# Five engine queues of one kernel, the same instructions in another order

## The reference

```python
    x = L0_attn_x
    xn = _layernorm(x, axis=-1)
    s = _L0_attn_ref(xn, ...)        # Mamba: in_W, conv of 4, silu, dbc, softplus, scan over 256 steps, 16 states, silu gate, out_W
    g = _silu(_L0_ffn_ref(xn, ...))  # six layers:
    #   x = attn_layer(shift_tokens(x), Wqkv, ...) + x   16 heads of 64, l2norm of q and k, rotary, windows of 32
    #   x = ffn_layer(shift_tokens(x), ...) + x          layer norm, W1, a * gelu(gate), W2
    x = x + s * g
```

## Time and profile before

| | us |
|---|---|
| median of 3 runs | 1926.24 (1923.84 to 1934.32) |
| the profiled execution | 1930.3 |
| its span, first to last instruction | 1928.5 |
| busy PE / DVE / POOL / ACT in the span | 1756.7 / 1596.1 / 1527.8 / 1252.5 |

### The profile page before, as it was taken

The page is one execution under the profiler, slowest core; times in us unless marked ns, Lnnn a source line. Parts: engine busy times, 40 slices in busy tenths (PEclk is TensorE's granted clock), DMA queues, the critical chain, the costliest instruction groups (busy, mean ns, idle before and its releaser), DMA issues. The chain is left out here.

```text
span 1928.5 us, 73996 instructions
## 1 busy us (share of the span) xinstructions
PE 1756.7 (91%) x30944; PEld 999.4 (52%) x30944; DVE 1596.1 (83%) x2736; ACT 1252.5 (65%) x2339; POOL 1527.8 (79%) x1348
## 2 busy tenths in 40 slices
PE   3798999999999999999999999999999999999862
PEld 1355555555555555555555555555555555555420
DVE  5777998888888897889988898889878798888536
ACT  3566676676676676776776676676766666766630
POOL 1765899878998789878998789888888689987640
PEclk9999999999999999999999999999999999999975
DMA  3114234153313334142332433342331534123321
GB/s 109 29 39 70 45 71 79 37 85 49 66 33 67 72 61 71 41 71 55 68 71 37 87 49 59 74 79 39 67 58 33 100 62 63 30 45 58 54 23 44
DMA packets 95607, 113.14 MB, mean 59 GB/s; under 512 B 42334, under 2 KB 61548, under 8 KB 95276
## 3 DMA queue, kind: packets, MB, share of 16 engines
q1 hardware_dynamic: 95276, 108.41, 31.1%
HBM read 19.22 MB, written 1.05 MB: 11 GB/s over the span
## 5 line engine op out<-in xcount | busy, mean ns | idle before, releaser
L1315 POOL TENSOR_TENSOR AB<-qc,qn 128x512 f32<-128x512 f32 x384 | 494.6, 1298 | 21.4 <-DVE qn L1109 21.4
L1326 POOL TENSOR_TENSOR AB<-AB,rinv 128x512 f32<-128x512 f32 x384 | 402.0, 1062 | 24.5 <-DVE rinv L1132 24.5
L559 PE MATMUL bank<-wqkv,XT 128*128 128x512 f32 x768 | 400.2, 614 | 12.2 <-DVE qn L1109 12.2
L1333 POOL TENSOR_TENSOR Pb<-Pb,p_rden 128x512 f32<-128x512 f32 x192 | 200.1, 1042 | 235.2 <-DVE p_rden L1153 234.1
L848 ACT ACTIVATE qkT<-bank 128x512 f32<-128x512 f32 x384 | 229.2, 597 | 209.3 <-PE bank L584 208.6
L1109 DVE TENSOR_TENSOR qc<-bank,rt 128x512 f32<-128x512 f32 x384 | 261.3, 680 | 123.4 <-ACT sq L839 108.9
L584 PEld LDWEIGHTS bank<-ident,AB 128*128 128x128 f32 x1536 | 181.7, 142 | 181.9 <-issue 119.3
L839 ACT ACTIVATE sq<-bank 128x512 f32<-128x512 f32 x384 | 228.1, 594 | 66.4 <-PE bank L559 57.3
L1109 DVE TENSOR_TENSOR qn<-bank,rt 128x512 f32<-128x512 f32 x384 | 261.4, 681 | 0.0
L584 PE MATMUL bank<-ident,AB 128*128 128x128 f32 x1536 | 241.5, 280 | 13.3 <-ACT qkT L848 6.2
L1116 DVE TENSOR_REDUCE ssq<-sq 128x8 f32<-128x512 f32 x384 | 251.2, 670 | 0.0
(11 more groups left out here) (137 smaller groups left out, 2657.3 us busy)
## 6 DMA issues: line engine op xcount, KB each, us to landing
V<-V SPq DMA_DIRECT2D x672, 64.0 KB, 2.1
rep<-du SPq DMA_DIRECT2D x64, 512.0 KB, 7.3
wqkv<-in_Wqkv SPq DMA_DIRECT2D x36, 256.0 KB, 3.7
XV<-XT SPq DMA_DIRECT2D x96, 64.0 KB, 2.8
wo<-in_Wo SPq DMA_DIRECT2D x6, 512.0 KB, 4.1
BC<-BC SPq DMA_DIRECT2D x8, 256.0 KB
w<-in_W SPq DMA_DIRECT2D x6, 341.0 KB, 3.2
BC<-BC SPq DMA_DIRECT2D x8, 128.0 KB
```

The costliest lines, as they stand in the source:

```text
L559: pe.matmul(R[u % 2][:], XT[:, s % NB, (u % 2) * P:(u % 2 + 1) * P], wqkv[:, (u // 2) * 512:(u // 2 + 1) * 512], start=True, stop=True).th ...
L1315: pool.tensor_tensor(AB[:, n % NAB, :], qc[:, u % 2, :], qn[:, u % 2, :], ALU.add).then_inc(rs_done, 1)
L1326: pool.tensor_tensor(o, o, r, ALU.mult).then_inc(nm_done, 1)
L1333: pool.tensor_tensor(Pb[:, g % 2], Pb[:, g % 2], r, ALU.mult).then_inc(pn_done, 1)
```

## The change

Each of the five loops gets its lines in another order, and `M_ORDER` follows. No call is added or dropped, no instruction, tile, buffer or semaphore changes. Some calls move by an iteration, so that their argument changes: `z_softplus` runs for step i-1 instead of i-2, the ACT call `z_copy_dbc` stands at the end of the list with i instead of further up with i-1, two `z_scan`, some `z_bu` and some `replicate` move likewise. Lines that the prediction speaks of, cut from the diff:

```diff
@@ M_ORDER @@
-M_ORDER = [("z_x", 0, -1, 6), ("z_dbc", 0, 1, 6), ("z_out", 0, 9, 6), ("z_g", 0, 5, 6), ("z_dup", 0, 1, 6),
+M_ORDER = [("z_dbc", 0, 1, 6), ("z_x", 0, -1, 6), ("z_dup", 0, 1, 6), ("z_out", 0, 9, 6), ("z_g", 0, 5, 6),
...
@@ block.sync @@
             for i in FIRST_TO_LAST:
+                replicate_bc(i - 3, 0)
+                spread(i, 0)
                 replicate(i - 4, 2)
-                next_qk(i, 1)
-                replicate(i - 7, 5)
-                replicate_bc(i - 3, 0)
-                replicate(i - 6, 4)
-                replicate_bc(i - 4, 4)
+                replicate_bc(i - 3, 1)
+                next_v(i, 0)
+                replicate_bc(i - 3, 2)
+                next_qk(i, 2)
+                replicate_bc(i - 3, 3)
                 replicate(i - 3, 0)
-                next_v(i, 0)
-                arrange_x(i + 2)
-                replicate(i - 7, 6)
-                replicate(i - 7, 7)
-                replicate_bc(i - 3, 1)
-                replicate_bc(i - 3, 2)
-                spread(i, 0)
-                next_qk(i, 2)
-                replicate(i - 5, 3)
-                replicate(i - 3, 1)
                 spread(i, 1)
                 next_qk(i, 3)
+                arrange_x(i + 2)
+                replicate_bc(i - 3, 4)
...
@@ block.tensor @@
             for i in FIRST_TO_LAST:
+                z_sum(i - 5, 0)
+                z_dbc(i - 1)
                 z_x(i + 1)
                 turn_p(i - 1, 3)
                 value(i, 1)
+                z_dup(i - 1)
                 value(i, 2)
                 turn(i, 0)
                 values_out(i - 1, 3)
+                turn(i, 1)
                 value(i, 3)
-                turn(i, 1)
-                qk(i + 1, 0)
-                qk(i + 1, 1)
                 scores(i, 0)
                 turn(i, 2)
-                z_sum(i - 5, 0)
+                qk(i + 1, 0)
+                z_out(i - 9)
                 w_out(i - 2, 0)
-                z_dbc(i - 1)
+                z_g(i - 5)
+                z_sum(i - 7, 4)
                 turn(i, 3)
-                z_out(i - 9)
-                z_g(i - 5)
+                qk(i + 1, 1)
+                scores(i, 1)
+                turn_p(i, 0)
                 qk(i + 1, 2)
-                z_dup(i - 1)
-                scores(i, 1)
+                z_sum(i - 5, 1)
+                turn(i, 4)
+                w_gelu(i - 3, 0)
+                values_out(i, 0)
                 qk(i + 1, 3)
                 w_out(i - 2, 1)
-                turn_p(i, 0)
-                w_gelu(i - 3, 0)
+                z_sum(i - 6, 2)
+                turn(i, 5)
+                w_gelu(i - 3, 1)
                 qk(i + 1, 4)
...
@@ block.vector @@
             for i in FIRST_TO_LAST:
+                z_scan(i - 8, 13)
+                z_scan(i - 6, 6)
                 res_ff(i - 4)
-                z_scan(i - 8, 13)
+                softmax(i, 0)
+                z_scan(i - 6, 7)
+                sum_p(i, 0)
                 rotate(i + 1, 0)
-                softmax(i, 0)
                 sum_squares(i + 1, 0)
+                softmax(i, 1)
+                rotate(i + 1, 1)
...
                 softmax(i, 2)
                 sum_squares(i + 1, 4)
                 gate(i - 3, 0)
-                sum_squares(i + 1, 5)
-                z_scan(i - 7, 10)
                 sum_p(i, 2)
...
                 sum_squares(i + 1, 7)
+                sum_p(i, 3)
                 guard_q(i + 1)
-                sum_p(i, 3)
                 rotate(i + 1, 7)
                 norm_q(i + 1)
...
@@ block.gpsimd @@
             for i in FIRST_TO_LAST:
-                z_hc(i - 6, 4)
+                normalise_p(i - 1, 3)
+                rotate_sum(i, 6)
                 normalise(i, 0)
                 normalise(i, 1)
-                z_bu(i - 7, 8)
+                normalise(i, 2)
+                normalise(i, 3)
+                z_bu(i - 4, 3)
+                z_hc(i - 7, 9)
+                z_hc(i - 6, 4)
+                normalise(i, 4)
+                z_bu(i - 5, 5)
+                z_delta(i - 2)
+                z_bu(i - 7, 10)
+                normalise(i, 5)
+                normalise(i, 6)
+                normalise_p(i, 0)
+                z_hc(i - 4, 0)
+                rotate_sum(i, 7)
+                z_bu(i - 5, 6)
+                rotate_sum(i + 1, 0)
                 z_hc(i - 8, 12)
-                rotate_sum(i, 6)
-                z_bu(i - 4, 2)
-                normalise(i, 2)
-                z_bu(i - 7, 9)
-                normalise(i, 3)
-                normalise(i, 4)
-                rotate_sum(i, 7)
-                z_bu(i - 7, 10)
+                z_bu(i - 8, 14)
+                z_bu(i - 3, 0)
                 z_hc(i - 6, 5)
-                normalise(i, 5)
-                rotate_sum(i + 1, 0)
-                normalise_p(i, 0)
+                z_bu(i - 7, 11)
                 rotate_sum(i + 1, 1)
...
+                rotate_sum(i + 1, 2)
+                z_hc(i - 8, 13)
+                normalise_p(i, 1)
...
-                z_delta(i - 2)
-                z_bu(i - 4, 4)
-                z_hc(i - 7, 11)
-                z_bu(i - 7, 13)
-                z_bu(i - 3, 0)
-                z_bu(i - 7, 14)
-                normalise_p(i, 3)
-                z_bu(i - 3, 1)
```

More of the change, by code:

```diff
@@ L788, in _ @@
+                w_gelu(i - 3, 1)
                 qk(i + 1, 4)
-                turn(i, 4)
-                values_out(i, 0)
-                w_gelu(i - 3, 1)
-                turn(i, 5)
-                qk(i + 1, 5)
+                w_gelu(i - 3, 2)
                 w_out(i - 2, 2)
-                w_gelu(i - 3, 2)
                 scores(i, 2)
                 turn_p(i, 1)
-                qk(i + 1, 6)
+                qk(i + 1, 5)
                 w_gate(i - 3, 0)
                 w_out(i - 2, 3)
+                qk(i + 1, 6)
@@ L1051, in _ @@
-                z_decay(i - 7, 9)
-                copy_p(i, 0)
-                gelu(i - 3, 0)
-                copy_qk(i, 4)
+                copy_v(i, 3)
+                copy_qk(i, 2)
+                expo(i, 0)
+                square(i + 1, 0)
+                copy_qk(i, 3)
+                z_copy_g(i - 5)
+                z_decay(i - 5, 4)
+                z_decay(i - 6, 8)
+                square(i + 1, 1)
+                z_decay(i - 7, 10)
+                copy_p(i, 0)
+                square(i + 1, 2)
@@ L1055, in _ @@
+                expo(i, 1)
+                copy_qk(i, 4)
+                z_exp_x(i)
+                gelu(i - 3, 0)
+                square(i + 1, 3)
                 copy_o(i, 0)
[L1056 removed]
                 gelu(i - 3, 1)
                 copy_qk(i, 5)
[L1059 to L1065 removed]
@@ L1428, in _ @@
-                z_bu(i - 8, 15)
-                rotate_sum(i + 1, 2)
-                rotate_sum(i + 1, 3)
-                normalise_p(i, 1)
-                z_hc(i - 7, 8)
-                z_bu(i - 5, 6)
-                z_hc(i - 7, 9)
-                z_hc(i - 8, 13)
-                z_hc(i - 6, 6)
-                z_hc(i - 4, 1)
-                z_bu(i - 7, 12)
-                z_hc(i - 6, 7)
-                z_hc(i - 5, 3)
-                z_hc(i - 8, 14)
-                normalise(i, 7)
@@ L1443, in _ @@
-                rotate_sum(i + 1, 4)
+                z_hc(i - 4, 1)
+                z_hc(i - 6, 6)
+                z_bu(i - 7, 12)
+                rotate_sum(i + 1, 2)
+                z_hc(i - 8, 13)
+                normalise_p(i, 1)
+                z_hc(i - 6, 7)
+                z_hc(i - 4, 2)
+                z_bu(i - 5, 7)
+                z_bu(i - 4, 4)
+                z_hc(i - 6, 8)
+                rotate_sum(i + 1, 3)
+                z_hc(i - 7, 10)
+                normalise(i, 7)
@@ L1444, in _ @@
+                z_bu(i - 8, 15)
+                z_bu(i - 6, 9)
+                z_bu(i - 3, 1)
+                z_bu(i - 5, 8)
+                z_bu(i - 3, 2)
+                rotate_sum(i + 1, 4)
+                z_hc(i - 8, 14)
+                normalise_p(i, 2)
+                z_silu_g(i - 5)
+                z_hc(i - 7, 11)
+                z_hc(i - 8, 15)
+                z_hc(i - 4, 3)
                 rotate_sum(i + 1, 5)
-                z_hc(i - 7, 10)
-                normalise_p(i, 2)
+                z_bu(i - 7, 13)
```

149 lines of the change are left out of this document (64 added, 85 removed).

## The result

The changed kernel takes 1953.7 us in the median of four runs, beside 1925.0 us for the kernel before on the same chip: a ratio of 1.0135, 95% interval 1.0092 to 1.0179. It is slower, by about 1.3%. I had forecast 1898 and faster, range 1866 to 1952; the time lies just above the range. (One of the four runs, at 2245 us and a mean granted clock of 0.74 where the others have 0.96, is in a slower state and is not in the ratio.) The profiled execution took 1945.6 us with a span of 1943.8, against 1930.3 and 1928.5.

A forecast was written before the change was run, and what follows sets the result against it. PE was taken as the bound, with waits between engines costing 93 of 1776 us. Gains of 19 (odd iterations), 7 (tables) and 2 make 28: profiled 1930.3 becomes 1902, median 1898, range 1866 to 1952.

The forecast's parts named there:

- part 4: DVE's new waits for expo and guess_q, about 0.8 us each: cost nothing; if not covered, up to 1.6 an iteration.
- parts 2 and 3: Earlier normalise_p before turn_p(i, 0): gain about 1 us phase 1, 0.5 phases 3, 5; transposes apart on bank T: 0.9 phase 3.
- no matter of order: PE's stops inside groups of matmuls, 23.9 us in 14 times, taken as something the order can't change.
- Part 1: Order made with distances between instruction starts instead of durations, which believe DVE 15% fuller: a reason for gain, no size.
- Part 5: rotate(1) on DVE waits for POOL's rt at layer changes; standing later gains 1 to 2 us at five changes, 7 us.
- Part 6: SP's links and POOL's earlier Mamba work: BC there at 14 us, z_bu(0) waits 1.5; cost 0 to 1 us in phase 3.
- The sum: 2.4 us in six iterations times 8 batches is 19, tables 7, a few more 2: gain 28 us.
- waits only move: Rival: odd iterations lose at the near-late chains what they gain elsewhere; time 1926, chance 0.16.
- BC comes late: Rival, slower side: links take 5 us each, POOL stands 9 us at z_bu(0), +61 us, time 1959; chance 0.28.

The follow-up runs named there:

- e3: Kernel before with thin refills: each refill of rep after the first four moves 16 KB instead of 512 KB; 1888.8 us.
- e4: Kernel after with thin refills: each refill of rep after the first four moves 16 KB instead of 512 KB; 1891.1 us.
- e13: Kernel before with SP's new list, each 512 KB refill of rep split into two 256 KB halves spread over the iteration; 1882.8 us.
- e14: Kernel after with each 512 KB refill of rep split into two 256 KB halves spread over the iteration; 1886.2 us.
- e15: Kernel after with thin refills, DVE's list edited: rotate(i + 1, 0) ahead of sum_p(i, 0), guard_q ahead of sum_p(i, 3); 1949.8 us.
- e18: Kernel after with thin refills, DVE's list edited only by putting guard_q ahead of sum_p(i, 3); 1898.8 us.
- e1: Kernel after with SP's list (all DMAs) in the old order, the computing engines' new orders kept; 2063.7 us.
- e2: Kernel before with SP's list alone in the new order; 1901.9 us, ratio 0.9863.
- e9: Kernel after with one line of SP's list moved: replicate(i - 5, 5) behind spread(i, 2), setting refills 4 and 5 apart; 1924.5 us.
- e5: Kernel after with 32 small matmuls ahead of PE's first work, shifting its instructions by half a page; 1949.3 us.
- e7: Kernel after with 96 small matmuls ahead of PE's first work, a shift of one and a half pages; 1973.8 us, 1947 less the later start.
- e16: Kernel before with SP's new list and its lines replicate(i - 5, 4) and replicate(i - 5, 5) exchanged, so both refills go out together; 1927.1 us.
- e17: Kernel after with each 512 KB refill of rep issued as two 256 KB halves, back to back at the whole one's place; 1920.3 us.

## Why the prediction was wrong, point by point

Two steps failed, and they add up. The first is part 4's "Cost nothing": PE lost there 2.3 us in six iterations, nearly all that parts 2 and 3 gained, and with the longer start it made 28 us of gain into none (e3 and e4, e13 and e14). The second is that the refills' bulk was left out of the reckoning as "no matter of order": it costs 54 us in the kernel after and 42 in the one before (profiled executions, against the thin kernels).

*What bounds the kernel.* "A part is no matter of order: PE stops inside a group of matmuls, released by nothing that the profile shows, 23.9 us in 14 times" set a row of 23.9 us aside. Its releaser stood in the page's table of DMA queues, and it is very much a matter of order: 0 to 42 us by where and how the refills are issued. Counted over all calls, the kernel before had 40.8 us of it, more than the 28 that I was about to gain. The sum of the stops is not itself what made the kernel slower, though: it fell to 33.2. What grew is all that the refills cost beside it.

*Part 1* gave a reason and no size; e3 and e4 give the size, none. The section "The DRAIN you can't avoid" of the Trainium skill's "VectorE: DVE Perf Modes", which I set against it, goes on: "A next op that is not held starts earlier". I left that out, so the 0.59 us of the earlier trace rows doesn't speak against the page; no run here tests when an instruction is held.

*Parts 2 and 3.* Right in size. To see it I compare e13 and e14, which have no stops. What PE loses before a call, beyond the call's own distance: before `turn_p(i, 0)` 2.1, 0.7 and 1.0 us in phases 1, 3 and 5 became 1.0, 0.0 and 0.4, and 0.2 came in phase 2; before `turn(i, 3)` 0.9 in phase 3 went. That is 3.1 in six iterations, where I had 2.9.

*Part 4.* Priced at nothing, and wrong. Most of what PE gained was lost again before `turn(i, 0)`: 0.5, 0.1, 0.2, 0.6, 0.4 and 0.6 us in phases 0 to 5, 2.4 in six iterations, against 0.1 with the old orders. The chain is in the timeline of iteration 28 of the kernel after, POOL first, then PE:

```profile
1098.63 1.27 POOL L1315 TENSOR_TENSOR AB<-qc,qn 128x512 f32<-128x512 f32 x1
1100.32 4.04 POOL L1326 TENSOR_TENSOR AB<-AB,rinv 128x512 f32<-128x512 f32 x4 [0.42 <-DVE rinv L1132]
```

```profile
1099.52 1.88 PE L575 MATMUL bank<-wqkv,XV 128*128 128x512 f32 x4
1101.51 0.63 PE L584 MATMUL bank<-ident,AB 128*128 128x128 f32 x4
```

`normalise(0)` waits 0.42 us for DVE's `norm_q` and ends 2.3 us after `turn_p(3)`, where PE has been through with `value(1)` and `value(2)` for 0.2 us. In the kernel before it ended 1.9 us after it. So `guard_q`, `guess_q` and `norm_q` at the end of DVE's list are next to the path, as `sum_p(0)` is at its head (e15), though DVE's share is only 83%. I had set its waits against its idle time in the iteration, and not against the time of whoever stood behind it. That "the two are only 0.4 apart" was in the text; it should have been the forecast. That the whole dependence is a loop through DVE that no exchange of neighbours shortens is my reading; e18 (no gain) fits it, but doesn't show it.

*Part 5.* DVE's wait for `rt` went from 9.5 to 3.6 us. Between e3 and e4, phase 1 got 4.5 us shorter in the iterations at a change of layer (7 and 31) and 2.0 to 3.6 in the others. So 1 to 2.5 at a change in phase 1, but nothing in phase 3 and a loss of 0.7 in phase 5 (iteration 23): 1 to 4 us in all rather than 7, and the first five iterations, 6 us longer in e4, took them.

*Part 6.* The links behaved: three in 5.1 us, as I had taken. Link 4 went out 12.4 us after the start, not 6.5, since it stands behind `spread(i, 1)`, whose V moves wait for ACT; but it landed in 3 us instead of 7.9. `z_bu(0)` began at 15.5 and had waited 2.1 us (I had 14 and 1.5). The cost was 0.7 us, inside my 0 to 1. What the part lacked is SP's other side: it asked when data arrives, and never when a buffer comes free. I wrote that earlier Mamba work "feeds `rep` in time". It also took away the wait that had kept two refills apart.

*The sum.* 28 us of gain became none: e3 and e4 differ by 2.4 us, which is the rival "waits only move" (1926), to which I gave 0.16. It said "each odd iteration loses there what it gains elsewhere"; in the traces the loss before `turn(i, 0)` is in the even ones as well. On that came the bulk of the refills: the profiled execution after is 54 us above its thin kernel, the one before 42. Stops are 31 and 36 us of these. That the new orders pay more for each stop is seen in iteration 29: 45.0 us from one `turn_p(3)` to the next against 36.1 in the thin kernel, 8.9 for one stop of 6.5, as PE goes on at clock 0.50 (stretches above). Phase 3 is 1.5 us longer than with thin refills, 12 us in eight batches, without stops. The rest, some 9 us, I can't assign. And these rows are of executions 15 us apart; the medians are 29 apart.

*The rivals.* "BC comes late" had the right side, which was luck, for it had not the right cause: its mechanism cost 0.7 us a batch here and 16 a batch in e1. My chance of 0.29 for slower rested on it alone. A rival that names PE's stops was missing.

## What to carry to other kernels

A row of waits that ends with "issue" inside a group of matmuls is not noise: look at what the DMA queues did in those microseconds, and whether a packet of the instruction queue was late. A wait in front of a bulk transfer may be what keeps it clear of the next one, so when an order makes an engine earlier, list the transfers that it releases. Cut transfers of 512 KB in two and put the halves where the queue has room, before searching orders of computation: on top of SP's new list that was worth 19 us with the old orders and 68 with the new ones, and the new orders of computation on top of it nothing (e14 is 3 us above e13). And an engine's share says nothing of the slack of one call: what decides is who stands behind it.

## What the runs showed of the hardware

PE's instructions reach it in packets of 16 KB, 256 instructions, one in 7 us at this kernel's pace, through the DMA engines that move data. While the refills in front fill these engines the packet does not begin, and PE goes on 2.2 to 2.8 us after it does (139 gaps in thirteen traces, none outside). Where a page border falls badly, one refill of 512 KB (5 us of full engines) goes with a stop of 1.9 to 2.7 us (phase 4 of the kernel after, e2 and e9), two in a row with anything from 0.8 to 7.0 us (phase 5 of the kernel after, e5, e7 and e16), and four halves in a row with 1.5 at most in phase 5 (e17). A shift by whole pages leaves the stops at their calls, a shift by half a page moves them. A small fp32 matmul of 32 columns is four instructions, and 64 of them took 27.5 us at the head of the program, 0.43 us each, so they filled PE's idle start and iteration 1 began 13.5 us later. PE's granted clock went from 1.00 (2.4 GHz) to 0.50 (1.2 GHz) during the 6.5 us stop and was still there in the first 2 us behind it.
